# Four layers on one core: Gelu written into its PSUM banks, a gating layer on centred maps, and f16 halves for the second wide attention's projections

## The reference

```python
x = x + L0_xattn(ln(x), ctx, ctx, mask, ...)   # 16 heads of 64, masked
x = x + L0_ffn(ln(x), tile_sigs, W, b)         # 8 maps, one chosen for each token
x = x + L1_xattn(ln(x), ctx, ctx, mask, ...)   # 16 heads of 8, masked
x = x + L1_ffn(...)                            # 16 heads of 8 on x itself, then 8 experts, 2 a token
x = x + L2_xattn(ln(x), ctx, ...)              # 16 heads of 64, no mask: the "second wide attention"
x = x + L2_ffn(...)                            # product of fp4-rounded x and weights
x = x + L3_xattn(...)                          # one head of 128, masked
x = x + L3_ffn(...)                            # 31 chosen tokens of 256

def L0_ffn(x, tile_sigs, W, b):
    scores = einsum('bsd,td->bst', x, sign(tile_sigs))      # 8 scores a token
    idx = argmax(scores)
    out = einsum('bsd,tde->bste', x, W) + b                 # all 8 maps
    return take(out, idx)                                   # the chosen one

def moe(x, ...):                                            # F = 512
    for e in range(8):
        h = gelu(x @ W1[e] + b1[e]) @ W2[e] + b2[e]
        out = out + combine[:, e] * h
```

## Time and profile before

| | |
|---|---|
| median of 3 runs | 559.14 us (557.73 to 559.91) |
| profiled execution | 557.98 us, span 556.2 us |
| PE busy | 516.7 us (93%), 4897 products |
| DVE busy | 433.5 us (78%) |
| ACT busy | 343.5 us (62%) |
| POOL busy | 259.2 us (47%) |
| transfers | 15.42 MB, 28 GB/s over the span |

### The profile page before, as it was taken

One profiled execution on the slowest core, in us unless ns is written; L12 is line 12 of the kernel. 1 busy time (PEld: TensorE's weight loads), 2 busy tenths in 40 slices (PEclk: granted clock), 3 DMA queues, 4 the chain that ended last, 5 costly groups with the idle time before them and its releaser, 6 DMA issues.

```text
span 556.2 us, 13261 instructions
## 1 busy us (share of the span) xinstructions
PE 516.7 (93%) x4897; PEld 295.2 (53%) x4897; DVE 433.5 (78%) x1206; ACT 343.5 (62%) x683; POOL 259.2 (47%) x282
## 2 busy tenths in 40 slices
PE   7899999998999899999999988989999999999996
PEld 3356666557843233343334566635566666964574
DVE  7999999996565988737857999777777776587663
ACT  4698888888226466645762966538777778522202
POOL 7957777777305510000112556207777777500100
PEclk9999999999999999999998999999999999999999
DMA  9760000001330000000000221000000000000000
GB/s 230 127 177 13 1 2 3 2 2 39 103 127 0 2 1 2 2 1 0 2 3 19 85 69 57 1 1 1 2 3 1 1 3 1 2 1 0 2 1 20
DMA packets 24083, 15.42 MB, mean 28 GB/s; under 512 B 8083, under 2 KB 22230, under 8 KB 23894
## 3 DMA queue, kind: packets, MB, share of 16 engines
q1 hardware_dynamic: 24022, 14.60, 9.8%
HBM read 14.33 MB, written 0.26 MB: 26 GB/s over the span
## 4 chain that ended last, share of the span: by engine, by line
PE 47%; DVE 20%; issue 17%; POOL 8%; ACT 6%; DMA 1%; DVEq 0%; POOLq 0%; ACTq 0%
PE pspair L506 7%; PE psO L521 4%; PE psS L492 4%; DVE Oall L1903 3%; PE pspair L695 3%; PE psO L720 3%; PE psM L468 3%; PE psM L464 2%; DVE nmx L1763 2%; PE pspair L492 2%; POOL PP L2350 2%; ACT PP L1290 2%; DVE Zt L1658 2%; POOL PP L2347 2%; PE pspair L943 2%
## 5 line engine op out<-in xcount | busy, mean ns | idle before, releaser
L506 PE MATMUL pspair<-ident,PP 128*128 128x128 f32 x512 | 82.0, 283 | 3.9 <-ACT PP L1290 3.7
L506 PEld LDWEIGHTS pspair<-ident,PP 128*128 128x128 f32 x512 | 54.2, 141 | 30.9 <-issue 21.9
L521 PE MATMUL psO<-V,PP 128*128 128x64 f16 x1536 | 65.7, 193 | 2.6 <-DVE Oall L1699 2.0
L1665 DVE TENSOR_TENSOR PP<-pspair,PP 128x512 f16<-128x512 f32 x64 | 44.0, 687 | 29.7 <-ACT PP L1274 29.7
L521 PEld LDWEIGHTS psO<-V,PP 128*128 128x128 f16 x1536 | 60.2, 98 | 9.0 <-DVE PP L1665 2.9
L1353 ACT ACTIVATE PP<-pspair 128x1024 f32<-128x1024 f32 x48 | 46.5, 1021 | 24.7 <-PE pspair L706 24.5
L2336 POOL TENSOR_TENSOR ln_rs<-ln_ve,minus_half 128x4 f32<-128x4 f32 x10 | 10.3, 1028 | 103.7 <-DVE ln_ve L1556 100.5
L2347 POOL TENSOR_TENSOR PP<-acc,one 128x512 f16<-128x512 f32 x32 | 33.3, 1042 | 37.0 <-ACT acc L1272 37.0
L1290 ACT ACTIVATE PP<-scores_m,nm 128x512 f32<-128x512 f32 x64 | 46.5, 726 | 5.7 <-DVE nm L1649 5.7
L2347 POOL TENSOR_TENSOR PP<-y_sb,one 128x512 f16<-128x512 f32 x32 | 33.3, 1041 | 18.8 <-ACT y_sb L1272 18.8
L2350 POOL TENSOR_TENSOR PP<-acc,PP 128x512 f16<-128x512 f32 x32 | 37.1, 1160 | 2.5
(11 more groups left out here) (571 smaller groups left out, 1268.2 us busy)
## 6 DMA issues: line engine op xcount, KB each, us to landing
W<-in_L_ffn_W SPq DMA_DIRECT2D x16, 256.0 KB, 2.8
bigw<-in_L_xattn_w_q SPq DMA_DIRECT2D x2, 512.0 KB, 7.8
bigw<-in_L_xattn_w_kv SPq DMA_DIRECT2D x1, 1024.0 KB, 7.4
V<-in_ctx SPq DMA_DIRECT2D x1, 512.0 KB, 4.2
bigw<-in_L_xattn_w_v SPq DMA_DIRECT2D x1, 512.0 KB, 5.5
mask_b<-in_mask_BxS_ff SPq DMA_DIRECT2D x1, 512.0 KB, 7.3
bigw<-in_L_xattn_w_k SPq DMA_DIRECT2D x1, 512.0 KB, 6.0
bigw<-in_L_xattn_w_o SPq DMA_DIRECT2D x1, 512.0 KB, 4.4
```

The lines of the kernel that those rows point to most:

```text
L506: mm = pe.transpose(bank[f"T{j % 2}"][:, k * P:(k + 1) * P], Pb[j % 4][:, k * P:(k + 1) * P], ident[:])
L521: mm = pe.matmul(bank["O"][:, (j % UPH) * a.dv:(j % UPH + 1) * a.dv], (PTH, PTL)[ppart][j % 4][:, k * P:(k + 1) * P], (VH, VL)[vpart][:, b ...
L1665: dve.tensor_tensor(PTL[j % 4][:, 0:a.keys], ps[:, 0:a.keys], PTH[j % 4][:, 0:a.keys], ALU.subtract).then_inc(free[f"T{j % 2}"], 1)
```

## The change

Four parts. (1) `project` takes f16 triples for L2x too, except for the first K0. Their halves come from POOL: context, key weights and query weights in six steps, each behind one spread of L1x (`l2x_half`), the input's halves (X16) after its turn. L2x's input is turned into XT[0] and no longer XT[1]. As wk16 and wq16 now live until L2x's last projection, SP loads mask_i and amask behind that one. (2) In the MoE the Gelu writes back into the bank that it reads; the cast and DVE's subtraction read the bank, and the subtraction frees it. (3) In L0f DVE only subtracts the mean and takes the factor 1/deviation into the gating row (pr8); the turned input is kept as f16 halves, the 8 maps as f16 halves that POOL forms after L0x, and the 8 products are f16 triples. Key and value products, the turn of the mask and the signatures' turn change places and banks, spare products are dropped, and three small DVE copies go to L1x (`small_loads`). (4) ACT's Sin goes behind the MoE, and a table warm-up with Exp goes.

```diff
-                if a.mask and (what, i, k) != ("K0", 0, 1):
+                if (what, i, k) != ("K0", 0, 1):
                     if (i, k) == (0, 1):
-                        pe.wait_ge(sem("L0x.halves"), 6 if what == "Q" else 4)
+                        pe.wait_ge(sem("L0x.halves"), (6 if what == "Q" else 4) if a.mask else (13 if what == "Q" else 10))
...
         def pe_signatures(pe):
             pe.wait_ge(sem("L0f.sign"), 1)
-            ps = take(pe, "L0f.sigT", "O")
+            ps = take(pe, "L0f.sigT", "S3")
...
+            for h, b in enumerate(("M", "S2")):
+                ps = take(pe, f"L0f.xt{h}", b)
+                for t in range(2):
+                    pe.wait_ge(sem("L0f.xn"), 2 * h + t + 1)
+                    mm = pe.transpose(ps[:, t * P:(t + 1) * P], XN[1][:, 2 * h + t, :], ident[:])
+                mm.then_inc(full[b], 1)
+            pe_l1x_values(pe, 0)
...
-                pe.matmul(ps[:], XT[1][:, t * P:(t + 1) * P],
-                          route_w[:, 4 * half:4 * half + 4, :].rearrange("p e d -> p (e d)"),
-                          start=True, stop=True).then_inc(full[f"S{n % 4}"], 1)
+                for m, (xpart, wpart) in enumerate(PARTS):
+                    mm = pe.matmul(ps[:], X16[:, xpart, t * P:(t + 1) * P], wk16[:, wpart, half * 512:(half + 1) * 512],
+                                   start=(m == 0), stop=(m == 2))
+                mm.then_inc(full[f"S{t}"], 1)
+            pe_onehot_rows(pe, "L0f", route_b)
+            pe_l1x_mask(pe)
             pe_early_keys(pe, range(2, 8))
...
-                pe.wait_ge(sem("moe.hlow"), NF * (2 * i + k2 + 1))
+                for k in range(NF):
+                    emptied(pe, f"moe.h{k}", 2 * i + k2)
...
-                            act.wait_ge(sem("moe.hlow"), NF * (e - 1) + k + 1)
-                        nc.scalar.activation(Pb[k][:], ps[:], ACT.Gelu, bias=cols[:, bass.ds(e * NF + k, 1)])\
-                            .then_inc(free_of(f"moe.h{k}"), 1)
+                        nc.scalar.activation(ps[:], ps[:], ACT.Gelu, bias=cols[:, bass.ds(e * NF + k, 1)])\
+                            .then_inc(sem("moe.gelu"), 1)
...
-                    dve.tensor_tensor(HT16[k2][:, 1, k, :], Pb[k][:], HT16[k2][:, 0, k, :], ALU.subtract)\
-                        .then_inc(sem("moe.hlow"), 1)
+                    dve.tensor_tensor(HT16[k2][:, 1, k, :], bank[at[f"moe.h{k}"][0]], HT16[k2][:, 0, k, :], ALU.subtract)\
+                        .then_inc(free_of(f"moe.h{k}"), 1)
...
+                ln_stats(X)
+                for t in range(NT):
+                    dve.tensor_scalar(XN[1][:, t, :], X[:, t, :], ln_mv[:, t, 0:1], None, ALU.subtract)\
+                        .then_inc(sem("L0f.xn"), 1)
...
+            pool.wait_ge(sem("ld.L0f"), 2 * 16)
+            route_flat = route_w.rearrange("p e d -> p (e d)")
+            for b, c in enumerate(halves):
+                split(wk16[:, 0, c], wk16[:, 1, c], route_flat[:, c], "L0.vsplit", b + 3)
...
-            spreads(L1X)
+            def l2x_half(k):
+
+                c = halves[k % 2]
+                if k < 2:
+                    split(ctxTm16[:, 0, c], ctxTm16[:, 1, c], ctxT[:, c], "L0x.halves", k + 7)
+                elif k < 4:
+                    split(wk16[:, 0, c], wk16[:, 1, c], bigw[:, 1, c], "L0x.halves", k + 7)
+                else:
+                    split(wq16[:, 0, c], wq16[:, 1, c], bigw[:, 0, c], "L0x.halves", k + 7)
+
+            pool.wait_ge(sem("ld.L2"), 2 * 16)
+            spreads(L1X, l2x_half)
...
+            emptied(pool, "L2x.xt")
+            split(X16[:, 0, :], X16[:, 1, :], XT[0][:], "L0x.halves", 13)
             pool_attention(L2X)
```

More of the change, by code:

```diff
@@ L840, in pe_l1x_kv, with pe_l1x_values, pe_l1x_mask @@
             emptied(pe, "L1x.wT")
-            pe_context_kv(pe, "L1x", sqT[:, 1, :], sqT[:, 2, :])
-            ps = take(pe, "L1x.mask", "T1")
+            for g in range(2):
+                pe_one(pe, f"L1x.k{g}", f"S{g}", sqT[:, 1, :], ctxT[:, g * 512:(g + 1) * 512])
+        def pe_l1x_values(pe, g):
+            b = f"T{g}"
+            ps = take(pe, f"L1x.v{g}", b)
+            for k in range(4):
+                c = 4 * g + k
+                mm = pe.matmul(ps[:, k * P:(k + 1) * P], ctxT[:, c * P:(c + 1) * P], sqT[:, 2, :], start=True, stop=True)
+            mm.then_inc(full[b], 1)
+        def pe_l1x_mask(pe):
+            ps = take(pe, "L1x.mask", "T0")
             pe.wait_ge(sem("mask"), 1)
@@ new lines, in pe_l0f @@
+            pe_l1x_values(pe, 0)
+            emptied(pe, "L0f.sigT")
+            for h in range(2):
+                emptied(pe, f"L0f.xt{h}")
+            ps = take(pe, "L0f.sc", "M")
+            for t in range(NT):
+                for h in range(2):
+                    mm = pe.matmul(ps[:, t * E:(t + 1) * E], X16[:, h, t * P:(t + 1) * P], signT[:],
+                                   start=(h == 0), stop=(h == 1))
+            mm.then_inc(full["M"], 1)
+            pe.wait_ge(sem("L0.vsplit"), 4)
@@ L1438, in _ @@
             act_copy(act, "L1x.wT", sqT[:, 0:4, :].rearrange("p k d -> p (k d)"))
-            act_context_kv(act, "L1x")
-            ps = filled(act, "L1x.mask")
-            nc.scalar.copy(maskT.rearrange("p k q -> p (k q)"), ps.bitcast(BF16)).then_inc(free_of("L1x.mask"), 1)
-            act_copy(act, "L0f.xt", XT[1][:])
+            act_l1x_key(act, 0)
+            for h in range(2):
+                act_high(act, f"L0f.xt{h}", X16[:, 0, h * 256:(h + 1) * 256], n=256)
+            act_l1x_key(act, 1)
+            act_l1x_values(act, 0)
+            act_l1x_values(act, 1)
             ps = filled(act, "L0f.cT")
@@ L1446, in _ @@
             for n in range(8):
+                if n == 2:
+                    ps = filled(act, "L1x.mask")
+                    nc.scalar.copy(maskT.rearrange("p k q -> p (k q)"), ps.bitcast(BF16)).then_inc(free_of("L1x.mask"), 1)
                 act_repeated_k(act, Kaug, "L1x", n // 2, n % 2)
+            act_wide_values(act, "L2", range(0, 2))
             act.wait_ge(sem("ld.short"), 16 * len(SHORT))
@@ L1474, in _ @@
             act_moe(act)
+            act.wait_ge(sem("L3f.angle"), 1)
+            nc.scalar.activation(ang2[:], ang[:], ACT.Sin).then_inc(sem("L3f.trig"), 1)
             act_wide_values(act, "L2", range(13, 2 * NC))
@@ L1585, in copy, with low @@
                 dve.tensor_copy(dst, ps[:, 0:n]).then_inc(free_of(name), 1)
-            def low(name, dst, high, bias=None, scale=None):
-                ps = filled(dve, name)
+            def low(name, dst, high, bias=None, scale=None, n=512):
+                ps = filled(dve, name)[:, 0:n]
                 dve.wait_ge(sem(f"high_{at[name][0]}"), highs[name])
@@ L2368, in pool_attention, with spreads @@
                 run(pool, a, rounds)
-            def spreads(a):
+            def spreads(a, meanwhile=None):
                 n = a.name
@@ L2595, in _ @@
                     expert_W2(e, k2)
+            filled(sp, "L2x.proj", L2X.per * (NPAIR - 1) - 1)
+            sp.dma_start(mask_i[:], A["mask_BxS2_ik1"].rearrange("b s -> (b s)").partition_broadcast(P))\
+                .then_inc(sem("ld.mask_i"), 16)
+            for b in range(B):
+                sp.dma_start(amask[:, 2 * b:2 * b + 2, :],
+                             A["L3_ffn_attention_mask"][b, 0, 0:S, 0:S].rearrange("(q p) s -> p q s", p=P))\
+                    .then_inc(sem("ld.amask"), 16)
             for b in range(B):
```

107 lines of the change are left out of this document (50 added, 57 removed).

## The result

The changed kernel takes 553.0 us (median of 7 runs, 551.48 to 555.61) against 559.05 for the one before (7 runs on the same chip, 557.73 to 559.91): a ratio of 0.9899, 95% interval 0.9872 to 0.9926. That is 6.05 us faster, where 8.0 were forecast (551.1, range 546.5 to 555.5); the time lies within the range, but 8.0 lies outside the interval, which is 4.1 to 7.2 us. The profiled execution has a span of 551.1 us against 556.2.

The account below looks back on a forecast made before the run. TensorE, busy 93% of the span, was taken to bound the kernel, with VectorE counting where TensorE waits for it. Terms 3.9 + 2.5 + 1.5 + 0.1 = 8.0 us, from 559.1 to 551.1; range 546.5 to 555.5.

Parts of the forecast that it names:

- L2x: Second wide attention: 14 Q and K1 projections as f16 triples each save 0.28 us, K0's saving vanishes in a wait: 3.9 us.
- MoE: Mixture of experts: Gelu in its PSUM bank keeps VectorE's subtraction at 0.69 us, two TensorE stalls go: net 2.5 us.
- Sin: Between the turn of L1f's input and its query: one ScalarE table load less, mostly covered by spare products: 0.1 us.
- head: First feed-forward L0f: centred turn and f16 halves save 3.6 us on VectorE, of which 1.5 us remain at L1x.
- Rival B: MoE: VectorE sets the pace and TensorE's hidden products wait for it; term 0 to -2, time 553.6 to 555.6; 15%.
- its loss: L0f: POOL's splits of W slow VectorE's mask casts and row add: 1.5 us less 0.9 of slack, 0.6 net.
- rival D: L0f up to L1x's rounds: dropped spare products let TensorE's clock fall and stay low, 12 us slower, 563; 5%.
- a short fall: TensorE's clock in L0f: a brief drop costs 1.2 us and stays within the range (552.3).
- I cost them at nothing: L1x: six POOL pairs of splits for L2x between the spreads, covered by POOL's 37.6 us of waiting: 0 us.

## Why the forecast was 2 us too high

| term | forecast | without clock falls | from |
|---|---|---|---|
| L2x | 3.9 | 3.98 | 99.01 - 95.03 |
| MoE | 2.5 | 2.77 | 106.50 - 103.73 |
| Sin | 0.1 | 0.28 | 106.78 - 106.50 |
| head, from L0x's first turn | 1.5 | 1.6 | 150.3 - 148.7 |
| L1x's rounds | 0 | -0.69 | 64.39 - 65.08 |
| sum | 8.0 | 7.9 | |
| more clock falls | 0 | -1.9 | the rest to 6.05 |

The profiles close the sum without the medians: their spans differ by 5.07 us, and 7.9 less 2.9 for the changed kernel's two falls (below) is 5.0.

**L2x** came out as worked: 14 products count, K0's six lie ahead of PE's wait for POOL, which went from 2.4 to 3.3 us. **MoE**: the place of the operand is the cause (some 2.7 of 2.77 with the waits left as changed). Rival B is refuted, VectorE kept pace. The Trainium skill (GPSIMD Engine Reference, Key points) holds VectorE instructions with two SBUF inputs for contended; this case's rows agree, 1751 ns against 692. **Sin**: I had taken six spare products to cover all but 0.1 us of it; it was 0.28.

**Head**: right without a fall, its loss included: the two mask casts beside POOL's splits of W took 1.40 us more, where I had 1.5. The part that I priced as an aside failed: rival D stood for a long stay at the low clock, at 5%, and a short fall was named as 1.2 us within the range, for which no row stood, but it should have been in the sum. The falls in the head cost 1.3 to 1.5 us in L0x and 1.2 to 1.5 in L0f, 2.9 together in the changed kernel's profile. How often falls come can be read from the mean clock of each timed run: a fall takes 3.4 us at half, so 0.003 of the mean over the 550 us. Before has 1.000 (557.66 to 558.23 us) or mostly 0.997 (558.9 to 559.6), so one fall costs it some 1.3 us; in its profile it cost nothing. The changed kernel has 0.996 to 0.988, one to four. With 550.0 for no fall (557.9 - 7.9; its profiled execution gives 552.83 - 2.9 = 549.9), its median carries 3.0 us of falls, that of before 1.1: the missing 1.9.

Where they come from can only be counted, in one profile for each kernel:

| place | pause of PE | profiles with a fall behind it |
|---|---|---|
| L0f | spare products dropped | 5 of 8, one of them at 164 us |
| L0f | with spare products, as before or three put back | 0 of 5 |
| ahead of L1x's first turn of maxima | 1.4 us | 6 of 7 |
| the same | 0.7 us, fed or gone | 0 of 6 |

So rival D's mechanism did come, as short falls and not as a long stay. That spare products keep a fall away is likely from these counts and is not shown for one place alone: the run that fed L0x and L1x has no fall in L0f either, where nothing was fed. The 1.40 us that PE waits ahead of L1x's first turn, for L1802, are the other lost term again: the same two instructions held by POOL cost 0.69 themselves, and behind the pause that they make stands, in the six, a fall of 1.1 to 1.6 us (L1x's rounds 66.17 to 66.71 with, 65.08 without). **L1x's rounds** stood in no term. "I cost them at nothing" was said of the new splits, and these did cost nothing. What I hadn't looked at is that an unchanged chain of POOL's splits shifts against three unchanged small VectorE instructions when the head shifts.

Open: why the fall at 28 to 31 us comes in four of the eight profiles with the changed head and an unfed L0x, and never in the two with the old one. The code up to there is the same. Two profiles are too few to call it a difference, and nothing here tells what sets it off beyond the pause of 2.25 us, which all of them have.

## To carry to other kernels

Before an order is changed, list the small VectorE instructions of SBUF operands on a chain and look at what POOL does beside them: a sum that moves a stage by a microsecond moves them under another split. Try spare products in PE's pauses ahead of dense work (here those of 1.4 and 2.25 us; they cost 0.2 us in L0x), and when an edit removes spares, put falls of the clock into the sum and not only into the range. The fed kernels still have single executions at a mean clock of 0.983. Where a saving vanishes in a wait, the engine that is waited for is the next edit: POOL's 2.2 us of keys in a pair, moved to two engines that read the bank, gave 3.5 us over the stage measured here, twice what K0's products alone could have (1.7).

## What the runs showed of the hardware

- Small VectorE instructions on SBUF alone (a scalar operation, a cast, and those with two inputs) that began behind the start of a POOL product ended when that product did: 128x8 in 0.83 and 1.01 us, 0.17 and 0.20 without; 128x32 in the MoE's gate in 0.69 to 0.98, 0.19 without. Two that began with a POOL product, within 0.01 us, took their 0.19, and so did the gate's reductions with one input. Large ones are stretched (the mask casts in L0f 0.86 and 1.38 us, 0.42 before). With an operand in PSUM none of L1941's was held (692 ns at most in 32). POOL is held the other way round too (2.64 us for 1.04).
- A fall of TensorE's granted clock to half lasts 3.4 us in all records. Its cost depends on the place: 1.3 to 1.5 in L0x, 1.2 to 1.5 in L0f at 150 to 154 us and 0.7 at 164, 1.1 to 1.6 in L1x's rounds. In the MoE it is 0.9 to 1.1 when the fall begins 5 to 6.4 us behind the first hidden product (five profiles), and nothing when it begins within 0.2 us of it (at 297.3, 302.8 and 303.0 us), where PE has time to spare.
- ScalarE's Gelu from PSUM into the same bank has medians of 0.66 and 0.69 us (at most 0.77), no more than to SBUF (0.69).
